# Attention in steps of two pairs of heads, on one core: scores and transposes of two pairs side by side

## What is computed

```python
q = (x @ wq).reshape(b, n, H, DH).transpose(0, 2, 1, 3)
k = (ctx @ wk).reshape(b, j, H, DH).transpose(0, 2, 1, 3)
v = (ctx @ wv).reshape(b, j, H, DH).transpose(0, 2, 1, 3)
sim = jnp.einsum('bhid,bhjd->bhij', q, k) * SCALE
sim = jnp.where(mask[:, None, None, :], neg, sim)
attn = jax.nn.softmax(sim, axis=-1)
out = jnp.einsum('bhij,bhjd->bhid', attn, v)
return out.transpose(0, 2, 1, 3).reshape(b, n, INNER) @ wo + bo
...
a = attention(x, x, tgt_mask, sa_wq, sa_wk, sa_wv, sa_wo, sa_bo)
x = layernorm(x + a, ln1_g, ln1_b)
a = attention(x, enc_output, src_mask, ca_wq, ca_wk, ca_wv, ca_wo, ca_bo)
x = layernorm(x + a, ln2_g, ln2_b)
```

## Time and profile before

| | |
|---|---|
| median of three runs | 1227.9 us |
| the profiled execution | 1228.4 us, of which the span of the instructions is 1226.6 us |
| TensorE matmuls | 1211.9 us busy, 99% |
| TensorE weight loads | 1163.3 us, 95% |
| VectorE, ScalarE, GpSimd | 981.8, 874.9, 681.2 us: 80, 71, 56% |

### The profile page before, as it was taken

How to read it: one execution, slowest core, us unless ns; L and a number is a source line. 1 busy time by engine, 2 the same in 40 slices (tenths; PEclk the granted TensorE clock), 3 DMA queues, 4 the chain that set the end, 5 groups by cost and what they waited for, 6 DMA issues and landing times.

```text
span 1226.6 us, 31369 instructions
## 1 busy us (share of the span) xinstructions
PE 1211.9 (99%) x10444; PEld 1163.3 (95%) x10444; DVE 981.8 (80%) x2674; ACT 874.9 (71%) x2259; POOL 681.2 (56%) x1089
## 2 busy tenths in 40 slices
PE   8999999999999999999999999999999999999998
PEld 6899999999999999999999999999999999999998
DVE  6888888988989988888888889854554888888854
ACT  6988888878887888888888788543433677767732
POOL 5766656656678855555565477887624033432231
PEclk9999999999999999999999999999999999999999
DMA  6060000000000002200000010111013677788722
GB/s 198 4 248 19 18 3 19 10 11 19 7 22 27 2 27 110 91 27 28 2 28 28 2 36 12 35 41 47 1 64 122 190 262 252 251 257 277 236 69 78
DMA packets 72207, 97.46 MB, mean 79 GB/s; under 512 B 5488, under 2 KB 52464, under 8 KB 72048
## 3 DMA queue, kind: packets, MB, share of 16 engines
q1 hardware_dynamic: 70512, 91.25, 22.9%
q0 software_dynamic: 1536, 4.20, 1.1%
HBM read 81.01 MB, written 14.42 MB: 78 GB/s over the span
## 4 chain that ended last, share of the span: by engine, by line
PE 84%; DVE 6%; ACT 5%; issue 3%; DMA 1%; SPq 0%; DVEq 0%; ACTq 0%
PE ps_pj L52 9%; PE ps_pj L54 9%; PE ps_pj L53 9%; PE ps_t L970 8%; PE ps_s L960 8%; PE ps_pv L983 8%; PE ps_aux L54 4%; PE ps_aux L52 4%; PE ps_aux L53 4%; ACT probs L1294 4%; PE ps_s L54 4%; PE ps_s L53 4%; PE ps_s L52 4%; PE ps_pv L54 2%; PE ps_pv L52 2%
## 5 line engine op out<-in xcount | busy, mean ns | idle before, releaser
L669 POOL TENSOR_SCALAR probs<-probs,inv 128x256 f32<-128x256 f32 x512 | 235.7, 479 | 220.9 <-DVE inv L1543 220.2
L1294 ACT ACTIVATE probs<-scores,nb 128x256 f32<-128x256 f32 x512 | 253.7, 497 | 16.5 <-DVE nb L1533 16.0
L1533 DVE CUSTOM_DVE_ANT_0 scores<-ps_s,maskf 128x256 f32<-128x256 f32 x512 | 186.7, 420 | 54.1 <-PE ps_s L960 51.7
L1301 ACT ACTIVATE probs_t_hi<-ps_t 128x512 fp32r<-128x512 f32 x256 | 150.7, 589 | 99.7 <-PE ps_t L970 99.6
L1547 DVE TENSOR_TENSOR probs_t_lo<-ps_t,probs_t_hi 128x512 fp32r<-128x512 f32 x256 | 172.8, 675 | 0.4
L970 PE MATMUL ps_t<-ident,probs 128*128 128x128 f32 x1024 | 139.9, 279 | 0.6 <-POOL probs L669 0.6
L52 PE MATMUL ps_pj<-xq_hi,wq_lo 128*128 128x256 f32 x448 | 138.1, 308 | 0.1
L983 PE MATMUL ps_pv<-probs_t_lo,v_stack 128*128 128x256 f32 x512 | 130.3, 287 | 1.1 <-issue 1.0
L983 PE MATMUL ps_pv<-probs_t_hi,v_stack 128*128 128x256 f32 x512 | 127.7, 282 | 0.0
L970 PEld LDWEIGHTS ps_t<-ident,probs 128*128 128x128 f32 x1024 | 109.7, 141 | 17.8 <-POOL probs L669 0.9
L54 PE MATMUL ps_pj<-xq_hi,wq_hi 128*128 128x256 f32 x448 | 126.2, 282 | 0.0
(11 more groups left out here) (275 smaller groups left out, 4439.5 us busy)
## 6 DMA issues: line engine op xcount, KB each, us to landing
raw<-in_L_ffn_W SPq DMA_DIRECT2D x90, 512.0 KB, 4.9
slot_rows<-hin SPq DMA_DIRECT2D x3, 768.0 KB, 6.1
rows<-in_x SPq DMA_DIRECT2D x8, 256.0 KB, 2.7
after_self<-rows SPq DMA_DIRECT2D x8, 256.0 KB, 2.1
rows<-after_self SPq DMA_DIRECT2D x8, 256.0 KB, 2.7
cin<-in_ctx SPq DMA_DIRECT2D x8, 256.0 KB, 3.0
...
```

The source lines that it names most:

```text
L669: last = pool.tensor_scalar(PR[:, h, t, :], PR[:, h, t, :], inv[:, h, t:t + 1], 1.0, ALU.mult, ALU.mult)
L1294: last = act.activation(PR[:, h, t, :], SM[:, h, t, :], ACT.Exp, bias=nb[:, h, t:t + 1], scale=-1.0, accum_out=sums[:, h, t:t + 1])
L1301: act.activation(flat(PT[0][:, i % 2, h, :, :]), ps_t[h][:, :], ACT.Copy).then_inc(t_hi, 1)
L1533: last = dve.tensor_tensor_reduce(SM[:, h, t, :], ps_s[h][:, t * S:(t + 1) * S], maskf[:, i // PAIRS % 2, :], -SCALE, -LOWEST, ALU.add, AL ...
```

## The change

Attention goes in steps `k` of two pairs (`TURNS_OF_TWO` = 63, four to a turn), i = 2k. TensorE makes the scores of pairs i+2 and i+3 one behind the other and the transposes of pairs i+1 and i+2 one behind the other. Scores of odd pairs go to the `ps_t` banks, and their turned probabilities to the `ps_s` banks (`scores_bank`, `turned_bank`). The masked maxima are written to, and the exponentials taken in place in, one of three `probs` buffers; `nb`, `sums` and `inv` are double. On VectorE `join_pair(i-1)` stands ahead of the masked maxima of the step. The tables of late weights count steps and give most steps two pieces, and `load_ctx` of turn 11 is issued ahead of the loads of the dense weights.

The events of the projection banks, and the tables of late weights:

```diff
     return u // B
 
 
+def turn_rows(k):
+
+    u = k // STEPS_PER_TURN + 1
+    if u < NTURN and k % STEPS_PER_TURN == 0 and layer_of(u):
+        return ("xc", u)
+    if u < NTURN and k % STEPS_PER_TURN == 1:
+        return ("xq", u)
+    return None
+
...
+        if 2 * k + 5 < NPAIR:
+            order.append(("qk", 2 * k + 5))
+        if turn_rows(k) is not None:
+            order.append(turn_rows(k))
     return {what: m for m, what in enumerate(order)}
 
 
-CTX_AT, ROWS_AT, FIRST_ROWS_AT = 2, 4, NPAIR - 2
+STEPS_PER_TURN = PAIRS // 2
+TURNS_OF_TWO = NPAIR // 2 - 1
 EVENT = bank_events()
-
-
...
-AHEAD = [("v", 1), ("q", 2), ("k", 2)]
-PIECES_IN = [{0: [("v", 2)], 1: [("q", 3), ("k", 3)], 2: [("o", 0)], 3: [("v", 3)], 4: [("o", 1)], 5: [("o", 2)], 6: [("o", 3)]},
-             {0: [("q", 0)], 1: [("k", 0), ("v", 0)], 2: [("q", 1), ("k", 1)], 3: [("v", 1)],
-              6: [("q", 2), ("k", 2)], 7: [("v", 2), ("o", 0)], 8: [("q", 3)], 9: [("k", 3), ("o", 1)],
-              10: [("v", 3), ("o", 2)], 11: [("o", 3)]},
-             {0: [("q", 0)], 1: [("k", 0), ("v", 0)], 2: [("q", 1), ("k", 1)], 3: [("v", 1)],
-              6: [("q", 2)], 7: [("q", 3), ("o", 0)], 8: [("o", 1)], 9: [("o", 2)], 11: [("o", 3)],
-              12: [("k", 2), ("v", 2), ("k", 3), ("v", 3)]}]
-PIECES_AT = {base + at: pieces for base, plan in zip(BASES, PIECES_IN) for at, pieces in plan.items()}
+AHEAD = [("v", 1), ("q", 2), ("k", 2), ("q", 3)]
+STARTS = (0, 26, 58)
+PIECES_IN = [{0: [("k", 3), ("v", 2), ("o", 0)], 1: [("v", 3), ("o", 1)], 2: [("o", 2)], 3: [("o", 3)]},
+             {0: [("q", 0), ("k", 0)], 1: [("q", 1), ("v", 0)], 2: [("k", 1), ("q", 2)], 3: [("k", 2), ("v", 1)],
+              4: [("q", 3), ("v", 2)], 5: [("k", 3), ("o", 0)], 6: [("v", 3), ("o", 1)], 7: [("o", 2)], 8: [("o", 3)]},
+             {0: [("q", 0), ("k", 0)], 1: [("v", 0), ("q", 1)], 2: [("k", 1), ("q", 2)], 3: [("v", 1), ("q", 3)],
+              4: [("o", 0)], 5: [("o", 1)], 6: [("o", 2)], 7: [("o", 3)], 8: [("k", 2), ("v", 2), ("k", 3), ("v", 3)]}]
+PIECES_AT = {start + at: pieces for start, plan in zip(STARTS, PIECES_IN) for at, pieces in plan.items()}
 
 
 def set_of(i):
 
-    return sum(i >= base for base in BASES[1:])
+    return sum(i >= start for start in STARTS[1:])
 
 
 LATE = [(0, kind, q) for kind, q in AHEAD] + [(set_of(j), kind, q) for j in sorted(PIECES_AT) for kind, q in PIECES_AT[j]]
 LATE_COUNT = {piece: n + 1 for n, piece in enumerate(LATE)}
 LATE_FIRST = sum(1 for piece in LATE if piece[0] == 0)
 LATE_SECOND = sum(1 for piece in LATE if piece[0] <= 1)
-SHARED_PIECES = PIECES_AT[NPAIR + 4]
+SHARED_PIECES = PIECES_AT[TURNS_OF_TWO + 3]
 
 FRONT = 5
```

Buffers, banks and the loads on SP:

```diff
         OT = at("heads_t_hi", 140 * KB, [P, 4, S], F32R), at("heads_t_lo", 148 * KB, [P, 4, S], F32R)
-        SM = at("scores", 152 * KB, [P, 2, ST, S])
-        PR = at("probs", 156 * KB, [P, 2, ST, S])
+        PR = [at(f"probs{r}", (152, 156, 132)[r] * KB, [P, 2, ST, S]) for r in range(3)]
         XQ = [(at(f"xq{r}_hi", (160 + 4 * r) * KB, [P, KC, S], F32R), at(f"xq{r}_lo", (162 + 4 * r) * KB, [P, KC, S], F32R))
               for r in range(2)]
         XC = [(at(f"xc{r}_hi", (168 + 4 * r) * KB, [P, KC, S], F32R), at(f"xc{r}_lo", (170 + 4 * r) * KB, [P, KC, S], F32R))
...
         mhalf = little("mhalf", [P, ST])
-        nb, sums, inv = (little(n, [P, 2, ST]) for n in ("nb", "sums", "inv"))
+        nb, sums, inv = (little(n, [P, 2, 2, ST]) for n in ("nb", "sums", "inv"))
...
         gathered, added, stored = [sem(f"gathered{q}") for q in range(TT // 2)], sem("added"), sem("stored")
+
+        def scores_bank(i, h):
+            return (ps_t if i % 2 else ps_s)[h]
+
+        def turned_bank(i, h):
+            return (ps_s if i % 2 else ps_t)[h]
 
...
@@ -585,7 +582,7 @@
                 sp.dma_start(slot_rows[first * P:(first + n) * P, :].rearrange("(p r) d -> p (r d)", r=n), zeros[:, 0:n * D])\
                     .then_inc(zeroed, 16)
             for u in range(NTURN):
-                if u + 1 < NTURN and layer_of(u + 1):
+                if u + 1 < NTURN and layer_of(u + 1) and u != B + 2:
                     load_ctx(u + 1)
                 if u == NTURN - 1:
                     for n in range(3):
@@ -595,6 +592,7 @@
                     if u + 2 < NTURN:
                         load_rows(u + 2)
                 if u == B + 1:
+                    load_ctx(u + 2)
                     sp.wait_ge(late_lo, LATE_SECOND)
                     sp.sem_inc(sp_gate, 1)
                     for k, (w, landed) in enumerate(zip(dense_weights, [third_in[k] for k in KINDS] + [w3_in])):
```

GpSimd's order:

```diff
-                    lo_of_pair(i - 2)
-                split_late(i)
-                if p == (6 if u == 0 else 0):
+            normalise(1, 0)
+            normalise(1, 1)
+            late_low(0, *AHEAD[3])
+            for k in range(TURNS_OF_TWO):
+                i = 2 * k
+                u, p = k // STEPS_PER_TURN, k % STEPS_PER_TURN
+                normalise(i + 2, 0)
+                normalise(i + 2, 1)
+                if k >= 1:
+                    lo_of_pair(i - 1)
+                if p == 1 and u + 1 < B:
+                    norm_input(u + 1)
+                if p == 2 and u >= 1:
+                    norm_output(u - 1)
+                normalise(i + 3, 0)
+                lo_of_pair(i)
+                if k == 0:
+                    for kind, q in PIECES_AT[0][:2]:
+                        late_low(0, kind, q)
+                elif set_of(k - 1) > 0 and k < TURNS_OF_TWO - 1:
+                    split_late(k - 1)
+                normalise(i + 3, 1)
+                if k == 0:
+                    late_low(0, *PIECES_AT[0][2])
+                elif set_of(k) == 0:
+                    split_late(k)
+                elif k == TURNS_OF_TWO - 1:
+                    split_late(k - 1)
+                if p == 2 and u >= 1:
+                    affine_output(u - 1)
+                if p == (3 if u == 0 else 0):
                     residual(u)
-                if p == 1 and u + 1 < NTURN:
+                if p == 0 and u + 1 < NTURN:
                     build_mask(u + 1)
-                if p == 2 and u + 1 < B:
-                    norm_input(u + 1)
-                if p == 4 and u >= 1:
-                    norm_output(u - 1)
-                if p == 5 and u >= 1:
-                    affine_output(u - 1)
-                if i == PAIRS - 2:
+                if k == STEPS_PER_TURN - 1:
                     pool.memset(hin[:, :, :, :], 0.0).then_inc(zero_ready, 1)
+            lo_of_pair(NPAIR - 3)
```

The waits of `scores` and `transpose_probs`:

```diff
                 pe.wait_ge(pj_lo, EVENT[("qk", i)] + 1)
-                wait(pe, max_ready, 2 * i)
+                if i == 2:
+                    pe.wait_ge(max_ready, 2)
+                elif i > 2:
+                    pe.wait_ge(t_lo, 2 * (i - 2))
...
-                wait(pe, t_lo, 2 * (i - 1) + h + 1)
+                if i == NPAIR - 1:
+                    pe.wait_ge(t_lo, 2 * (i - 2) + h + 1)
+                else:
+                    pe.wait_ge(max_ready, 2 * (i + 1) + h + 1)
                 for j in range(ST):
                     for t in range(ST):
-                        last = pe.transpose(ps_t[h][:, j * S + t * P:j * S + (t + 1) * P],
-                                            PR[:, h, t, j * P:(j + 1) * P], ident[:, :])
+                        last = pe.transpose(turned_bank(i, h)[:, j * S + t * P:j * S + (t + 1) * P],
+                                            PR[i % 3][:, h, t, j * P:(j + 1) * P], ident[:, :])
                 last.then_inc(t_done, 1)
 
             def attend(i):
```

TensorE's order:

```diff
-            for i in range(NPAIR + 3):
-                if i == 1:
-                    project_qk(i + 2)
-                if i + 1 < NPAIR:
-                    scores(i + 1)
-                if i == 0:
-                    project_qk(i + 2)
-                if i == FIRST_ROWS_AT:
+            scores(1)
+            project_qk(2)
+            transpose_probs(0, 0)
+            transpose_probs(0, 1)
+            project_qk(3)
+            for k in range(TURNS_OF_TWO):
+                i = 2 * k
+                scores(i + 2)
+                scores(i + 3)
+                if i + 4 < NPAIR:
+                    project_qk(i + 4)
+                attend(i)
+                project_v(k + 1)
+                if k == TURNS_OF_TWO - 1:
                     transpose_first(0)
-                if i == NPAIR - 1:
-                    up_dense(0, 0)
-                    up_dense(0, 1)
-                if i < NPAIR:
-                    transpose_probs(i, 0)
-                    transpose_probs(i, 1)
-                if i >= 2 and i + 2 < NPAIR:
-                    project_qk(i + 2)
-                if i >= 4 and i % 2 == 0:
-                    output(i - 4)
-                    output(i - 3)
-                extra = extra_event(i)
-                if extra is not None and extra[0] != "h":
-                    {"v": project_v, "xq": transpose_rows, "xc": transpose_ctx}[extra[0]](extra[1])
```

(106 more changed lines are left out.)

169 lines of the change are left out of this document (61 added, 108 removed).

## The result

The changed kernel takes 1253.3 us (median of four runs, 1251.7 to 1253.8), the kernel before 1228.0 us beside it: a ratio of 1.020, with a 95% interval of 1.019 to 1.0215. It is 25 us slower. The forecast was 1240, with a range up to 1249: the sign was right, the forecast size half of what came. The profiled execution took 1251.7 us, 23.4 more than the profiled one of before.

What follows compares the result with a forecast made beforehand. A chain through ScalarE and VectorE was to bound attention: 62 x 11.10 = 688.2 plus 54.4 gives 742.6 us for 729.3, +13.3; with -0.5 and -1, +11.8 on 1228.4, taken as 1240 us, range 1213 to 1249.

Steps and rivals of the forecast that it cites:

- the ring: Attention's step from ScalarE's last bank copy through VectorE's qk_lo, join and maximum to ScalarE's exponentials and next copy: 11.10 us.
- extras: Work added to the 62 steps: statistics 23.1, low parts 14.0, casts 11.9, weight copies 2.6, TensorE's route 2.8; 54.4 us.
- What bounds the kernel before: Attention runs at TensorE's pace, busy 299.2 of 300 us; VectorE's late work was taken up by idle time before the maxima.
- TensorE's switches: Changes of matmul kind in attention lose 0.38 us per two-pair step instead of 0.68; TensorE's step falls from 11.50 to 11.20.
- the way through TensorE: Where two plain steps follow each other, the path via scores, attend, cross and join adds 0.2 us a turn, 2.8 us.
- The first turns: In attention's first four steps, seven weight copies on ScalarE add 2.6 us.
- Start and end: Start: scores(1) no longer waits for the maxima, -0.5 us; after pair 126's scores: one projection less, partly given back, -1.
- Waits to be seen: Signs in attention: TensorE waits at ps_s for qk_lo 30 us and more; ScalarE's probs wait for nb 1.5 us a step.
- Turns: Eight pairs of attention take 47.3 us in the first layer, 46.9 in the second, 49 to 50 with casts.
- A: Rival, faster: in attention TensorE keeps the pace and VectorE's late work is hidden, 1209 us; chance 0.09.
- The rule of the fullest engine: Optimize the fullest engine first, here TensorE by its weight loads: its saved time would show in full, about 1209 us.
- C: Rival, slower by more: residual_sum and GpSimd's full steps find no cover, +9 and +5, up to 1252 us; chance 0.14.

Runs made afterwards that it cites:

- e9: The kernel before with the statistics of attention's rows taken over 32 of 256 columns: 1224.8 us, ratio 0.9969.
- e5: The kernel before with attention's statistics made twice: 1248.1 us, ratio 1.0156.
- e6: The changed kernel with only VectorE's statistics and casts moved behind the first two masked maxima of the next step: 1223.5 us, ratio 0.9962 to the kernel before.
- e4: The changed kernel with attention's statistics made twice: 1272.0 us.

## Why the prediction was half right

The direction and the chain were right; the measured time lies above the range. The step that failed is the length of the ring: 11.10 us in the prediction, 11.28 in the trace, 11.2 us over the 62 steps. The stretch behind the last step (4.6), the start (1.0) and the distance between profiled runs and medians (2) come on top, 1.4 stays undivided, and extras that were put 6.6 too high take part of it back: 13.6 us in all.

- **What bounds the kernel before**: right. But "what VectorE did late was taken up by its idle time" was too generous: e9 shows a third of it exposed, e5 that nothing was left over.
- **TensorE's switches**: right. In the changed kernel the scores of the second pair follow at 0.12 (603.69 to 603.81), the first projection comes 0.21 behind the last scores (604.48 to 604.69) with 0.22 behind it, and TensorE's own step, seen in e6, is 11.22 (11.20 forecast).
- **The ring of 11.10**: the mechanism was right, the size was not: it is 11.28, and this is the term that failed most. By its parts, in the first plain step of a turn (ScalarE, VectorE):

```profile
591.10 0.62 ACT L1319 ACTIVATE qk_hi<-ps_pj 128x512 fp32r<-128x512 f32 x1
591.75 0.69 DVE L1565 TENSOR_TENSOR qk_lo<-ps_pj,qk_hi 128x512 fp32r<-128x512 f32 x1
592.36 0.84 DVE L1609 TENSOR_TENSOR joined<-ps_pv,cross 64x256 f32<-64x256 f32 x2
593.24 0.42 DVE L1586 CUSTOM_DVE_ANT_0 probs<-ps_s,maskf 128x256 f32<-128x256 f32 x1
594.05 0.51 ACT L1329 ACTIVATE probs<-probs,nb 128x256 f32<-128x256 f32 x1 [1.72 <-DVE nb L1586]
```

  Copy to `qk_lo` 0.65 (0.61 forecast); `qk_lo` to join 0.61 (0.61); join to maximum 0.88 (0.87) and to the exponential 0.81 (0.81); ScalarE's chain, to the next copy at 602.38, 8.33 (8.20), two gaps of 0.12 and a heads copy that is 0.13 shorter than counted. Here ScalarE's second `cross` does run beside `qk_lo`, as forecast. In the plain step behind it, it does not: `cross` waits for TensorE's `attend`, whose last matmul starts at 602.78 and ends at 603.06, runs from 603.10 to 603.70, and the join waits for it, 0.70 behind `qk_lo`. This makes 11.37, and it is the way through TensorE, for which the forecast had 0.2 a turn; it is 0.09.
- **What stands in the ring**: right in kind and in place, somewhat high in size; read from the same copies, over the 62 steps. A statistic costs 12.19 - 11.28 = 0.91 (0.88 by e6, 0.87 by e4) where I had 1.05, and only 21 fall into these steps, as the last one comes behind the scores of pair 126: 19.1 us, for 23.1. A low part costs 12.78 - 12.19 = 0.59, for 0.61: 13.6 us for 23, for 14.0. The casts: 22 fall into the 62 steps, and the steps that hold them are 11.3 us longer than their like, for 11.9, though 3 to 4 us of that are clashes with GpSimd that I had not counted. The first turns: 2.9 us, for 2.6. The way through TensorE: 0.9, for 2.8.
- **The sum over 62 steps**: 62 x 11.28 = 699.4, where I had 688.2, and the extras come to 47.8 us for 54.4; 1.4 us of the 748.6 I can't divide. So +11.2, -6.6 and +1.4: 748.6 for 742.6. That the sum misses by 6 us only is in part luck, since the ring was too short and the extras too long. Of the 13.6 us between forecast (1239.7 as a median) and measured median these are 6.
- **Start and end**: wrong, by 1 and 4.6 us. At the end I counted one projection less, 1.4 us, and allowed 0.4 us of it for new waits. TensorE's timeline there has four waits with 4.7 us in all, of which these are the two longest (the others 0.78 and 0.56):

```profile
774.24 0.35 PE L1006 MATMUL ps_pv<-probs_t_lo,v_stack 128*128 128x256 f32 x1 [1.52 <-issue]
...
790.81 0.39 PE L52 MATMUL ps_aux<-wo_hi,heads_t_lo 128*128 128x256 f32 x1 [1.83 <-POOL heads_t_lo L687]
```

  The first is the late work once more: `attend` waits for the join behind the casts and statistics shown above. The rest of the difference, 2 us, is between profiled runs and medians: the changed kernel's profiled run was its fastest, 1.6 under its median (its mean clock was 1.000, that of the other three 0.999), that of before 0.4 over.
- **Waits to be seen**: `ps_s` for `qk_lo` with 30 us and more did not show; they stand at `ps_t`, the scores of the odd pairs, with 8.7 us. A loss of the forecast size is there all the same: 62 steps of 11.22 and 23 transposes of rows or context at 0.44 (their four and the slower first matmul behind) would be 705.8 us, so TensorE lost 43. The list of waits shows some 20 of it, the smaller entries included, since a gap counts only beyond the modelled end of a matmul (0.28 for a spacing of 0.12) and each restart costs about 0.1 more (0.19 to 0.22 to the next start, for 0.12). The waits of `ps_t` for GpSimd's probabilities (6.7 us) I had excluded ("over a microsecond late, so nothing").
- **Turns**: 47.3 forecast, 47.6 measured in the first layer; 46.9 and 47.3 in the second; with casts 49.2, 50.9 and 49.7, for 49 to 50.
- **Rivals**: A (TensorE keeps the pace) is what e6 comes near by moving the work, with 45.85 us a turn for TensorE's 45.3, not what the change did. The rule of the fullest engine, which the prediction took from the Trainium skill, would have given about 1209, and the runs speak against it here: TensorE's own step became shorter and the kernel slower. C had the size, 1252, but by another mechanism: no wait points to `residual_sum`, and of GpSimd's part the 6.7 us of waits and the 3 us of clashes are real.
